# Attention in two stages on one core: the values of an odd slot move behind its transposes and projection

## What is computed

```
x = x + _L0_attn_a_ref(_layernorm(x), Wq, Wk, Wv, Wpost)

def _L0_attn_a_ref(X, Wq, Wk, Wv, Wpost):
    Q = (X @ Wq).reshape(n, s, 16, 64)
    K = (X @ Wk).reshape(n, s, 16, 64)
    V = (X @ Wv).reshape(n, s, 16, 64)
    raw_attn = einsum('bshe,bthe->bsth', Q, K / 8)
    attn = softmax(raw_attn, axis=2)
    A = einsum('bsth,bthe->bshe', attn, V).reshape(n, s, 1024)
    return X + gelu(A) @ Wpost
```

## Time and profile before

| | |
|---|---|
| median of 3 runs | 3846.21 us (3840.87 to 3852.88) |
| profiled execution, its own time | 3842.12 us |
| its span, first to last instruction | 3840.3 us |
| TensorE busy | 3695.5 us, 96% of the span |
| VectorE busy | 2748.2 us, 72% |
| ScalarE busy | 2317.9 us, 60% |
| GpSimd busy | 1934.6 us, 50% |
| mean granted TensorE clock | 0.983 of full speed |

### The profile page before, as it was taken

The page is one execution under the profiler, slowest core; times in us unless marked ns, Lnnn a source line. Parts: engine busy times, 40 slices in busy tenths (PEclk is TensorE's granted clock), DMA queues, the critical chain, the costliest instruction groups (busy, mean ns, idle before and its releaser), DMA issues.

```text
span 3840.3 us, 65127 instructions
## 1 busy us (share of the span) xinstructions
PE 3695.5 (96%) x24194; PEld 2497.9 (65%) x24194; DVE 2748.2 (72%) x4367; ACT 2317.9 (60%) x4501; POOL 1934.6 (50%) x1219
## 2 busy tenths in 40 slices
PE   8999999999999999999999868999999999999987
PEld 6777777777777777777777654555555555555544
DVE  6766667666666766766666757888888888888762
ACT  5666656566566656556665426666666666666654
POOL 4555555555555555555555444555555554444412
PEclk9999999999999999999999879999999999999989
DMA  2000000000000000000000023333333333333220
GB/s 77 7 12 1 12 12 12 1 12 12 1 12 12 12 1 12 12 1 12 12 15 1 24 54 52 56 57 60 58 56 56 56 56 56 56 56 57 51 45 17
DMA packets 90920, 114.19 MB, mean 30 GB/s; under 512 B 10800, under 2 KB 64432, under 8 KB 90608
## 3 DMA queue, kind: packets, MB, share of 16 engines
q1 hardware_dynamic: 90608, 110.02, 14.3%
HBM read 33.43 MB, written 25.17 MB: 15 GB/s over the span
## 4 chain that ended last, share of the span: by engine, by line
PE 83%; DVE 11%; ACT 3%; issue 2%; POOL 1%; DMA 0%; SPq 0%; DVEq 0%; POOLq 0%; ACTq 0%
PE ps_o L624 12%; PE ps_s L593 10%; PE ps_t L606 8%; PE ps_t L216 7%; PE ps_o L700 5%; PE ps_t L735 5%; PE ps_m L606 4%; PE ps_s L673 4%; PE ps_t L726 4%; DVE max_b L1098 4%; PE ps_t L659 3%; PE ps_t L223 3%; PE ps_t L716 3%; PE ps_m L216 3%; PE ps_s L687 2%; PE ps_m L726 2%
## 5 line engine op out<-in xcount | busy, mean ns | idle before, releaser
L487 POOL TENSOR_TENSOR e_a<-e_a,recip 128x1024 f32<-128x1024 f32 x512 | 969.7, 1894 | 958.5 <-DVE recip L964 958.4
L778 ACT ACTIVATE e_a<-ps_s,neg_max 128x512 f32<-128x512 f32 x1024 | 694.4, 685 | 554.3 <-DVE neg_max L957 553.9
L820 ACT ACTIVATE et<-ps_s 128x1024 f32<-128x1024 f32 x512 | 523.6, 1023 | 373.1 <-PE ps_s L687 372.8
L1098 DVE TENSOR_REDUCE max_b<-ps_s 128x2 f32<-128x1024 f32 x512 | 622.7, 1217 | 161.6 <-PE ps_s L673 159.5
L957 DVE TENSOR_REDUCE neg_max<-ps_s 128x2 f32<-128x1024 f32 x512 | 622.7, 1216 | 69.4 <-PE ps_s L593 69.4
L624 PE MATMUL ps_o<-et_a,v_a 128*64 128x256 f32 x4096 | 501.8, 387 | 6.7 <-ACT et_a L785 1.5
L593 PE MATMUL ps_s<-raw_a 64*128 64x512 f32 x3072 | 427.8, 410 | 11.7 <-ACT e_a L778 11.5
L523 POOL TENSOR_TENSOR h_lo<-h,h_hi 128x512 fp32r<-128x512 f32 x256 | 333.5, 1318 | 168.3 <-ACT h_hi L864 168.3
L624 PEld LDWEIGHTS ps_o<-et_a,v_a 128*64 128x64 f32 x4096 | 280.3, 137 | 190.9 <-issue 77.4
L606 PE MATMUL ps_t<-ident,e_a 128*128 128x128 f32 x2660 | 395.5, 281 | 5.9 <-DVE xl L1141 5.8
L971 DVE COPY et_a<-ps_t 128x512 f32<-128x512 f32 x366 | 250.9, 687 | 204.3 <-PE ps_t L606 200.2
(11 more groups left out here) (197 smaller groups left out, 7439.0 us busy)
## 6 DMA issues: line engine op xcount, KB each, us to landing
q_stack<-roped_q SPq DMA_DIRECT2D x256, 64.0 KB
k_stack<-roped_k SPq DMA_DIRECT2D x256, 64.0 KB
x_a<-X SPq DMA_DIRECT2D x16, 512.0 KB, 3.8
X<-x_a SPq DMA_DIRECT2D x16, 512.0 KB, 2.9
x_ahead<-X SPq DMA_DIRECT2D x16, 512.0 KB, 3.9
X<-x_ahead SPq DMA_DIRECT2D x16, 512.0 KB, 4.3
q_stack<-roped_q SPq DMA_DIRECT2D x256, 32.0 KB
k_stack<-roped_k SPq DMA_DIRECT2D x256, 32.0 KB
```

The source lines that it names most:

```text
L487: nc.gpsimd.tensor_tensor(e_a[:, u % 5, :, :], e_a[:, u % 5, :, :], factor, ALU.mult).then_inc(e_normed, 1)
L778: ins = nc.scalar.activation(e_a[:, u % 5, h, :], ps_s[:, 2 * (u % 2) + h, :], ACT.Exp, bias=neg_max[:, u % 5, h:h + 1], accum_out=sums[:, ...
L820: nc.scalar.activation(et[:, v % 5, :, :], ps_s[:, 2:4, :], ACT.Exp)\
L1098: nc.vector.reduce_max(max_b[:, u // 4 % 2, :, u % 4], ps_s[:, score_bank(u):score_bank(u) + 2, :], AX.X, negate=True).then_inc(max_done, 1)
```

## The change

In odd slots TensorE's list had the values first, then the transposes, then the product. Now the transposes and the product come first and the values last. Even slots (scores, transposes, product) are as they were, and so are the last values at slot 512.

```
                     if slot < LAST_A:
                         if slot % 2 == 0 and 0 <= slot + LEAD < UNITS_ALL:
                             a_scores(slot + LEAD)
-                        if slot % 2 == 1 and 3 <= slot < UNITS_ALL:
-                            a_values((slot - 3) // 2)
                         if slot == UNITS_ALL:
                             a_values(UNITS_ALL // 2 - 1)
                         if 0 <= slot < UNITS_ALL:
                             a_transposes(slot)
                         for todo in todo_of.get(slot, []):
                             a_product(todo)
+                        if slot % 2 == 1 and 3 <= slot < UNITS_ALL:
+                            a_values((slot - 3) // 2)
```

## The result

The changed kernel takes 3966.22 us (median of four runs, 3962.57 to 3970.62), the kernel before 3847.34 in the same job: a ratio of 1.0308, with a 95% interval of 1.0296 to 1.032. It is 119 us slower; the forecast was slower by 141, at 3987, with a range of 3938 to 4042.

What follows compares the result with a forecast made beforehand. TensorE's list, run end to end, bounds the first stage. Net waits of 8.79 us a sequence, 141 us for 16, on 3842.1 give 3983; the median, 4.1 higher, gives 3987, range 3938 to 4042.

Steps and rivals of the forecast that it cites:

- What bounds: First stage: TensorE's list runs end to end, busy 2119 of 2140 us; any new wait lengthens it by its full length.
- The shape of the array: TensorE's tile-shape changes per pair of slots: four become three, saving 0.08 us a pair, 20 us at most.
- The middle value: One shape change saved per pair, 0.08 us, between two saved (another 20 us) and none.
- The ordinary pair: Slots 10 and 11: odd product waits 0.71 us for the even "qk" bank, 0.63 net; also slots 2, 14, 26, 30.
- the first rival: Freeing times stay, no earlier maximum: wait 0.30 us longer in eight "qk" pairs, 38 us more, 4025; chance 0.20.
- The special pairs: Even slots with other VectorE work, net us: 6 1.61, 18 0.99, 22 1.69, 16 0.64, 20 0.84, 4 0.19.
- the head roundings in slots 22 and 6: VectorE rounds two heads ahead of the subtraction: 1.80 us in slot 22, 1.11 in 6, each less 0.08 overlap.
- What costs nothing: Odd slot's transposes come 1.9 us earlier, with inputs ready and banks emptied in time; the values' waits get more time.
- The bare chain: Rival: VectorE's further work out of the way; eight "qk" pairs cost 0.63 us, others gain 0.08: 70 us, 3917; chance 0.10.
- The other side: Rival: "qk" banks free within 1.09 us, no pair waits, 20 us go: 3826; chance 0.04.

Runs made afterwards that it cites:

- the first experiment: Changed kernel with the values moved between transposes and product in odd slots: 3898.07 us, ratio 1.0128.
- the better order: Changed kernel, VectorE emptying the even slot's product before the next maximum in odd slots 5, 7, 17, 19, 21; with GpSimd's subtraction one slot later: 3911.35 us.
- the mixed version: Kernel before with values last in odd slots 1, 5, 13, 21, 29, VectorE's emptying first in 5 and 21, GpSimd's heads subtraction one slot later: 3822.32 us.
- the run without slot 23: Changed kernel with VectorE's emptying ahead of the maximum in odd slots 5, 7, 17, 19 and 21 only: 3963.63 us, ratio 1.0303.

## Why the prediction was right, and where it was off

**What bounds.** Right: TensorE's list ran end to end, and the new wait lengthened the stage by its length.

**The shape of the array.** The trace after has the two borders that could only be bounded. From the last pair of product matmuls to the transposes it takes 0.46 us (931.25 to 931.71), two steps of 0.23: no change of shape is paid. From the last pair of the values to the scores it takes 0.31 (927.47 to 927.78), where a step between pairs of the values is 0.22 (1.88 less 0.31, over seven): one is paid, some 0.09. The middle value of 0.08 us held; of the pairs without a wait those of slots 24 and 28 were 0.07 and 0.08 shorter, those of slots 12 and 0 0.14 and 0.17, which one border does not account for. The rule of the Trainium skill on the drain at a change of mode (TensorEngine Tiling, Tiling Modes) agrees: a border within one mode costs nothing here, one between modes 0.08 to 0.09 us. The 20 us that it would have given as the whole result show in the free pairs alone; the waits buried them.

**The ordinary pair.** Right in each step, and in the sum: 0.63 us net forecast; 0.63 to 0.66 measured in the pairs of slots 10, 14, 26 and 30, from scores to scores in both traces. The relief, a maximum that begins at 1.0 us and not at 1.35, came as worked out, which decides against the first rival.

**The special pairs.** Slots 18 and 20 were near: 0.90 and 0.93 for 0.99 and 0.84; slot 16 had 0.62 for 0.64, slot 4 0.29 for 0.19. The term that was mis-sized is the head roundings in slots 22 and 6: 1.69 and 1.61 net forecast, 0.96 and 1.24 measured. I carried the 1.80 us of the earlier trace rows over as the work of two roundings. It was not: GpSimd ran beside them in the trace before,

```profile
930.78 2.54 POOL L491 TENSOR_TENSOR heads_parts<-heads_a,heads_parts 128x512 fp32r<-128x512 f32 x2
...
932.13 1.47 DVE L1006 CAST heads_parts<-heads_a 128x512 fp32r<-128x512 f32 x1
```

and the first of the two lasted until just behind GpSimd's end at 933.32. In the changed kernel the slots are longer, the two meet otherwise, and the same place reads:

```profile
981.53 1.67 PE L593 MATMUL ps_s<-raw_a 64*128 64x512 f32 x12
...
982.94 2.52 POOL L491 TENSOR_TENSOR heads_parts<-heads_a,heads_parts 128x512 fp32r<-128x512 f32 x2
...
985.04 1.05 DVE L1006 CAST heads_parts<-heads_a 128x512 fp32r<-128x512 f32 x2
...
987.21 0.67 DVE L982 SCALAR_TENSOR_TENSOR raw_a<-ps_m,raw_a 128x512 fp32r<-128x512 f32 x1
...
987.93 0.66 PE L641 MATMUL ps_m<-ident,xn_a 128*128 128x128 f32 x4 [1.44 <-DVE raw_a L982]
```

The product of slot 23 starts 6.40 us after the scores of slot 22, not at 7.14. In slot 6 of the changed kernel the two roundings take 0.42 us each, where the first took 0.77 before. The two terms together were 1.1 us a sequence too large, 18 us of the 22 between forecast and result (141 and 119). The pair of slot 2 was 0.15 us better than forecast, a small rest. The sum took 16 like sequences, 7.5 us each as measured. The first cost 9.5 and the last, which has fewer products, 3.4; that these two nearly make up for each other is luck.

**What costs nothing.** The cover of the transposes held, but the first experiment shows how thin it was: with the maximum 0.32 us later, the second transposed fill is late and TensorE stops. I named that the banks were emptied in time and not what they hung on.

**The bare chain** as a rival (70 us) was wrong for the change itself, where VectorE's order and GpSimd add to it. The run that gave VectorE the better order and moved GpSimd away lands there: 64 us.

**The other side.** A bank free in time does turn the sign, as the mixed version shows, in pairs chosen for it: 15 us, with GpSimd's move taken off.

## What to carry to other kernels

Where two producers share a ring of banks, what stands between one fill and the next fill of the same bank is cover for the emptying: before work is moved out from there, add up the emptying chain with its hand-overs and compare it with what stays. The same move can be good in one slot and bad in the next, so try it by slot, with what stands in front of each. And a duration read from a row can hold another engine's time; before it goes into a sum, look for the same instruction elsewhere at its shortest.

## What the hardware showed that was not expected

VectorE's rounding of 128 by 512 from SBUF to SBUF is 0.42 us by itself; started beside a GpSimd instruction it lasts until shortly behind GpSimd's end (1.47 us in the row above, 2.09 for two in the run without slot 23). In the trace before, all 49 roundings that started beside one of GpSimd's multiplications or subtractions ended 0.28 to 0.34 us behind its end. VectorE's statistics for the layer norm were not held: in the changed kernel 30 of them started beside GpSimd and took the same 0.41 us as the others. Moving GpSimd took it away in slot 22 each time, and was worth 9.5 us on the kernel before and 52 us on the changed kernel with the better order on VectorE, where the wait and the fall of the clock went with it. The Trainium skill (GPSIMD Engine Reference, Specifications) states that GpSimd shares its SBUF interfaces with VectorE, with contention for VectorE's instructions in a two-port mode or with two SBUF inputs. The rows agree that there is contention, and show here that the rounding was held to the end of GpSimd's instruction; which mode it runs in no run here shows.

Waits of 0.2 to 1.5 us in 11 of the 16 pairs of a sequence left the granted clock at 1.00. Two longer ones in the first sequence of the changed kernel, 2.56 and 2.11 us, were followed by 0.57 and 0.51. In the run without slot 23 the 2.38 us were followed by 0.56 over the values of that slot, which took 1.2 us more. The same wait, 2.37 or 2.38 us, stands in slot 23 of 14 sequences of that run, and in three of them the clock stayed at 1.00: the pair then took 10.72 us, where it took 12.0 to 12.4 in the other eleven. So the length of the wait alone does not tell whether the clock falls. Such a price appears in none of the terms of a sum; it comes on top of the longest wait.
